# Gelu of the expert layer written to 32-bit buffers in SBUF in place of PSUM, and four buffers for its high and low halves

## The chip, the cores and the metric

The kernel runs on one core of one Trainium2 chip. The metric is the device time of one execution in microseconds. The profile's engines are TensorE (PE, with its weight loads shown apart as PEld), VectorE (DVE), ScalarE (ACT), GpSimd (POOL) and SyncE (SP, which here only issues DMAs).

## What is computed

The reference is a small hybrid of convolution and attention over an input of 4 batches, 128 channels and 32 x 32 positions, so 4 x 1024 tokens of 128 values. Cut to what matters:

```python
x = conv_attention(x, theta_w, phi_w, proj_w)          # softmax(theta x . phi x) applied to x, projected, added
t = tokens(x)                                          # 4 x 1024 tokens of 128
t = t + attention(layernorm(t), Wk, bk, Wq, bq, Wv, bv)
xf = layernorm(t)                                      # the expert layer
top_w, top_i = top_k(xf @ Wg + bg, 2)                  # two of eight experts for each token
for e in range(8):
    h = gelu(xf @ W1[e] + b1[e])                       # 128 -> 512
    out += w_dense[:, e] * (h @ W2[e] + b2[e])         # 512 -> 128
t = t + out
```

The change lies in the expert layer alone.

## The kernel before

Products are made with 16-bit operands: a 32-bit value is held as a high half (its 16-bit rounding) and a low half (what the rounding left), and the products of the halves are summed.

**Attention stage.** The first two thirds of the program run eight attention units, pipelined over steps. There DVE makes the low halves of the exponentials at line 1784 and line 1791 (`EL <- E, EH`: a 32-bit buffer in SBUF less a 16-bit buffer in SBUF), and at line 1860 low halves of weights from SBUF buffers. Towards its end POOL sends the normalised tokens to a buffer in memory (`zbuf`), sorted by expert: function `scatter`, line 605, one indirect DMA for each of 64 groups of 128 rows, whose row numbers (`posi`) lie in SBUF.

**Expert stage.** The tokens sorted by expert are worked through in 36 tiles, `j` from 0 to 35: the first 28 tiles (`WHOLE`) have 256 rows of one expert, the last 8 are pairs of half tiles of 128 rows, each with an expert of its own. For each tile

- SP loads the rows into one of eight buffers (`load_tile`, line 486);
- PE turns them (`rows_T`, line 1092), and ACT copies them to SBUF (`rows_T`, line 1241);
- PE makes the hidden layer (`hidden`, line 1116) in one of two PSUM buffers, `WIDE[0]` (named SC in the trace) and `WIDE[1]` (named PV);
- ACT applies Gelu in place in PSUM (line 1483) and then copies the result to the high half `hh` (line 1489; the trace shows it as line 1213, `EH <- SC` or `EH <- PV`);
- DVE makes the low half `hl` (`low_halves`, line 2038): the Gelu in PSUM less the high half in SBUF. I call this instruction the low of tile j;
- PE makes the output product (`output`, line 1135) in PSUM (MX), two tiles behind the hidden layer;
- DVE sums the parts of the product (`output`, line 2040; the reduction is line 2052) into one of 24 buffers, and makes the row numbers (`yid`, line 2048);
- POOL sends each half of 128 rows to its rows in memory (`ybuf`; function `put`, line 727, indirect DMA of line 731). I call one such DMA a put: two for each tile, 71 in all, as the last tile has one half.

**What sets the order.** Every engine runs a list that is written out by hand, and semaphores tie them. PE's list is `hidden(j)`, `output(j - 2)`, `rows_T(j + 2)`. ACT's is Gelu of j, high half of j, `rows_T(j + 2)`. DVE's is low of j, output of j - 2, and for j up to 12 some small instructions that make the tables of the next tiles (lines 1649 to 1720). POOL's is first the scatters of the last two batches, then the puts in the order of the tiles.

**Waits around the change.** `hidden(j)` writes over the PSUM buffer that low of j - 2 reads, so it waits for that low (`hl_ready`, line 1123). High and low halves have two buffers, so the high half of j and low of j wait for the output product of j - 2 (`y_full`, lines 1488 and 2034). `output(j)` on PE waits for low of j, and for the reduction of j - 2 (`y_ready`).

**The end.** SP loads the results back by parts (`load_outputs`, line 504): the first part once tiles 0 to 31 are written, the second with tile 32, and so on to tile 35. DVE and ACT weigh and add them (`mix_half`, line 2059, lines 2055 and 2068; `mix_quarter`), PE turns the sums, ACT copies and SP stores them.

Of the kernel before, what the change touches and what calls it, by code (L numbers as in the profile page):

```python
# [20 lines left out]
F32 = mybir.dt.float32  # L21
F16 = mybir.dt.float16
# [4 lines left out]
ACT = mybir.ActivationFunctionType  # L27
AX = mybir.AxisListType

P = 128  # L30
B = 4
S = 1024
T = S // P
# [6 lines left out]
WS = 64.0  # L40
HALF = 512
VW = P + 1
# [6 lines left out]
HC = HID // P  # L49
TR = 2 * P  # L50
# [9 lines left out]
NT = WHOLE + REST // 2  # L60
# [2 lines left out]
PADS = E + E  # L63
IN_BUFS = 8
Y_BUFS = 24


def build(nc, x, theta_w, phi_w, proj_w, Wk, bk, Wq, bq, Wv, bv, Wg, bg, W1, b1, W2, b2, out):
    ds = bass.ds
    with ExitStack() as ctx:  # L70
        def sb(name, shape, dt):
            return ctx.enter_context(nc.sbuf_tensor(name, shape, dt))
# [4 lines left out]
        def sem(name):  # L77
# [8 lines left out]
        ZN = ZZ[:, :, 2 * P:ROW].bitcast(I32)  # L86
        QK = sb("QK", [P, 3, 4, S], F16)
        QH, QL, KH, KL = (QK[:, :, j, :] for j in range(4))
        VH = sb("VH", [P, 4, T, VW], F16)
        VL = sb("VL", [P, 4, T, P], F16)  # L90
        EH = sb("EH", [P, 2, T, S], F16)
        EL = sb("EL", [P, 2, T, S], F16)
# [59 lines left out]
        EH0, EH1 = (EH[:, j].rearrange("p a b -> p (a b)") for j in range(2))  # L152
# [32 lines left out]
        Xg = Xw.rearrange("p (g d) -> p g d", g=E * HC)  # L185
        tin = EH0[:, 0:IN_BUFS * 2 * ROW].rearrange("p (b q r) -> p b q r", q=2, r=ROW)
        zT = EH0[:, IN_BUFS * 2 * ROW:IN_BUFS * 2 * ROW + 4 * TR].rearrange("p (b h r) -> p b h r", b=2, h=2)
        hh, hl = (EH1[:, at:at + 2 * HC * TR].rearrange("p (b r) -> p b r", b=2)
                  for at in (4 * TR, 4 * TR + 2 * HC * TR))
        y32 = [t.bitcast(F32)[:, TR * b:TR * (b + 1)].rearrange("p (q c) -> p q c", q=2)  # L190
               for t in (EL0, QK0[:, 8 * S:]) for b in range(t.shape[1] // (2 * TR))]
        yid = sb("yid", [P, Y_BUFS, 2], U32)
# [15 lines left out]
        WIDE = [t[:].rearrange("p b n -> p (b n)") for t in (SC, PV)]  # L208
# [75 lines left out]
        h_ready = sem("h_ready")  # L284
        hh_ready = sem("hh_ready")
        hl_ready = sem("hl_ready")
        y_full = sem("y_full")
# [452 lines left out]
        def _(pe):  # L740
            def mm(o, w, r, start, stop):
                return nc.tensor.matmul(o, w, r, start=start, stop=stop)  # L742
# [7 lines left out]
            for s in STEPS:  # L750
                u, a, m, v = roles(s)
# [364 lines left out]
            def hidden(j):  # L1116

                if j > 0 and listed_at(j, 0) % E == 0:
                    load_experts(listed_at(j, 0) // E)
                b = j % 2  # L1120
                pe.wait_ge(zt_ready, j + 1)
                if j >= 2:
                    pe.wait_ge(hl_ready, j - 1)
                for q in (None,) if j < WHOLE else halves(j):
                    e = expert(j, q)
                    r = slice(0, TR) if q is None else slice(q * P, (q + 1) * P)
                    for c in range(HC):
                        o_ = WIDE[b][:, c * TR:(c + 1) * TR][:, r]
                        w = ds(e * HID + c * P, P)
                        mm(o_, W1H[:, w], zT[:, b, 0, r], True, False)  # L1130
                        mm(o_, W1H[:, w], zT[:, b, 1, r], False, False)
                        last = mm(o_, W1L[:, w], zT[:, b, 0, r], False, True)
                last.then_inc(h_full, 1)

            def output(j):

                b = j % 2
                pe.wait_ge(hl_ready, j + 1)
                if j >= 2:
                    pe.wait_ge(y_ready, j - 1)  # L1140
                for q in halves(j):
                    if q == 0 or j >= WHOLE:
                        e = expert(j, q)
                        both = [W2HL[:, ds(e * HC + c, 1), :, :] for c in range(HC)]
                        mine = pick[:, ds(e, 1), :]
                    o_ = MX[:, b * HALF + q * TR:b * HALF + (q + 1) * TR]
                    for c in range(HC):
                        k = slice(c * TR + q * P, c * TR + (q + 1) * P)
                        if c < HC - 1:
                            mm(o_, hh[:, b, k], both[c], c == 0, False)  # L1150
                            mm(o_[:, 0:P], hl[:, b, k], both[c][:, :, 0, :], False, False)
                        else:
                            mm(o_[:, 0:P], hl[:, b, k], both[c][:, :, 0, :], False, False)
                            mm(o_[:, 0:P], mine, B2[:], False, False)
                            last = mm(o_, hh[:, b, k], both[c], False, True)
                last.then_inc(y_full, 1)

            pe.wait_ge(table_ready, 2)
# [16 lines left out]
            for j in range(2, NT):  # L1175
                if j == FIRST:
                    pe.wait_ge(table_ready, 4)
                if j == FIRST + SECOND:
                    pe.wait_ge(table_ready, 6)
                if listed_at(j, 0) // E == WHOLE // E:  # L1180
                    pe.wait_ge(table_ready, 8)
                hidden(j)
                if j == 2:
                    pe.wait_ge(last_logits_read, 1)
                    pe.wait_ge(wexp_lo, 2 * PAIRS)
                    pe.wait_ge(b2_ready, 1)
                    pe.wait_ge(picks_made, 2)
                if j == 3:
                    pe.wait_ge(rank_read, B)
                output(j - 2)  # L1190
                if j + 2 < NT:
                    rows_T(j + 2)
            for j in (NT - 2, NT - 1):
                output(j)


# [14 lines left out]
        def _(act):  # L1211
# [34 lines left out]
            for s in STEPS:  # L1246
                u, a, m, v = roles(s)
# [230 lines left out]
            def gelu(j):  # L1478
                b = j % 2
                act.wait_ge(h_full, j + 1)  # L1480
                r = slice(0, len(halves(j)) * P)
                h_, high = (o.rearrange("p (c r) -> p c r", c=HC)[:, :, r] for o in (WIDE[b], hh[:, b, :]))
                nc.scalar.activation(h_, h_, ACT.Gelu, scale=1 / WS).then_inc(h_ready, 1)

                act.wait_ge(h_ready, j + 1)
                if j >= 2:

                    act.wait_ge(y_full, j - 1)
                cp(high, h_).then_inc(hh_ready, 1)

            for j in range(NT):
# [30 lines left out]
        def _(dve):  # L1522
# [506 lines left out]
            def low_halves(j):  # L2029
                b = j % 2  # L2030
                dve.wait_ge(hh_ready, j + 1)
                if j >= 2:

                    dve.wait_ge(y_full, j - 1)
                r = slice(0, len(halves(j)) * P)
                h_, high, low_ = (o.rearrange("p (c r) -> p c r", c=HC)[:, :, r]
                                  for o in (WIDE[b], hh[:, b, :], hl[:, b, :]))
                nc.vector.tensor_tensor(low_, h_, high, ALU.subtract).then_inc(hl_ready, 1)  # L2038

            def output(j):  # L2040
# [49 lines left out]
            picks(B - 1)  # L2090
            for j in range(NT):
                low_halves(j)
                if j >= 2:
                    output(j - 2)
                if j == 0:
                    place(B - 1)
                    nc.vector.tensor_copy(padrow[:], start[:]).then_inc(pad_ready, 1)
                if j == 1:
                    not_done()
                    segment_ends(E)  # L2100
                    segments_past(SECOND, E)
                    segment_jumps(SECOND, E)
                if j == 2:
                    summed_past(FIRST, SECOND, E)
                    summed_jumps(FIRST, SECOND, E)
                    listed(FIRST, SECOND, E)
                if j == 3:
                    taken(SECOND)
                if j == 4:
                    counted_tiles(whole_tiles[:], ALU.is_gt, P, TR)  # L2110
                    counted_tiles(total[:], ALU.is_gt, 0, P)
                if j == 5:
                    third_tiles()
                    segment_ends(2 * E)
                if j == 6:
                    segments_past(THIRD, 2 * E)
                    segment_jumps(THIRD, 2 * E)
                if j == 7:
                    summed_past(FIRST + SECOND, THIRD, 2 * E)
                    summed_jumps(FIRST + SECOND, THIRD, 2 * E)  # L2120
                    listed(FIRST + SECOND, THIRD, 2 * E)
                if j == 9:
                    taken(THIRD, 2 * E)
                if j == 10:
                    last_halves()
                    segment_ends(2 * E)
                if j == 11:
                    segments_past(REST, 2 * E)
                    segment_jumps(REST, 2 * E)
                if j == 12:  # L2130
                    summed_past(WHOLE, REST, 2 * E)
                    summed_jumps(WHOLE, REST, 2 * E)
                    listed(WHOLE, REST, 2 * E)
                if j == 15:
                    weigh(1, slice(0, (B - 1) * T))
                    nc.vector.memset(spare[:], 0.0).then_inc(weighed, 1)
            for j in (NT - 2, NT - 1):
                output(j)
            for k in range(2 * (B - 1)):
                mix_half(k)  # L2140
# [28 lines left out]
```

## Time and profile before

| | us |
|---|---|
| median of three runs | 466.13 (466.06 to 467.18) |
| the profiled execution | 465.63 |
| its span, first to last instruction | 463.9 |

| engine | busy us | share of the span |
|---|---|---|
| PE (matmul) | 382.6 | 82% |
| DVE | 360.7 | 78% |
| ACT | 331.2 | 71% |
| POOL | 301.3 | 65% |

The shares are averages over the attention stage, the expert stage (first Gelu at 319.46 us of the span, last put issued at 442.24 us) and the end. The granted TensorE clock is 1.00 of full speed from 330 us to 438 us and 0.50 from 322 us to 326 us; these are its levels of 2.4 and 1.2 GHz. A line of the timeline gives the start, the duration, the engine, the line of the kernel, the operation, output and inputs by name, the shape, and in brackets how long the engine had been idle before it and what released it.

### The profile page before, as it was taken

Reading aid. Unit: us, or ns where it says so; the run is one execution under the profiler, and the core shown is the slowest. Engines: PE = TensorE matmul, PEld = TensorE weight load, DVE = VectorE, ACT = ScalarE, POOL = GpSimd, SP = SyncE. Lnnn points to the kernel's source line nnn. Section 1 sums busy time; section 2 is a strip of 40 time slices with the busy share of each in tenths; the row PEclk is TensorE's granted clock in tenths of the full one; section 3 lists DMA queues with packets and bytes.
Section 4 is the critical chain, followed back from the end, with each engine's and each line's share of the span. In section 5 each row is a group of like instructions: output and inputs, shape, how many; then the busy total and the mean of one; then the engine's idle time right before and its main releaser. Section 6 shows DMA issues by size and latency. Waiting matters only on the chain. (4 is left out here: it accounts for less than half of the span.)

```text
span 463.9 us, 12169 instructions
## 1 busy us (share of the span) xinstructions
PE 382.6 (82%) x3919; PEld 287.0 (62%) x3919; DVE 360.7 (78%) x1024; ACT 331.2 (71%) x650; POOL 301.3 (65%) x304
## 2 busy tenths in 40 slices
PE   4777679997999989999959677466999999999534
PEld 3443356675666756767737455464889899987422
DVE  3795789998889898989797289687898876655656
ACT  4687958785896867877748487459678888866553
POOL 9423834776877776575658857767777777775510
PEclk9997999998999999999999799888999999999955
DMA  6006022200000000002300010133244333331386
GB/s 217 10 12 172 2 46 91 95 3 2 0 2 1 2 1 2 1 2 78 105 7 27 29 36 30 48 88 99 71 116 112 107 92 103 100 94 46 81 273 244
DMA packets 31775, 30.67 MB, mean 66 GB/s; under 512 B 8678, under 2 KB 24953, under 8 KB 31721
## 3 DMA queue, kind: packets, MB, share of 16 engines
q1 hardware_dynamic: 27402, 21.05, 16.4%
q0 software_dynamic: 4320, 8.92, 5.8%
q8 instruction: 32, 0.52, 0.5%
q14 instruction: 21, 0.17, 0.1%
HBM read 17.87 MB, written 12.08 MB: 65 GB/s over the span
## 5 line engine op out<-in xcount | busy, mean ns | idle before, releaser
L1302 ACT ACTIVATE E<-SC 128x512 f32<-128x512 f32 x128 | 77.3, 604 | 44.1 <-PE SC L742 41.4
L742 PE MATMUL PV<-VH,EH 128*128 128x129 f16 x512 | 97.4, 229 | 5.9 <-DVE TOK L1803 5.9
L742 PE MATMUL SC<-QK 128*128 128x512 f16 x326 | 92.1, 389 | 9.3 <-ACT EH L1303 3.2
L742 PE MATMUL PV<-VH,EL 128*128 128x129 f16 x512 | 97.1, 226 | 0.0
L742 PE MATMUL PV<-VL,EH 128*128 128x128 f16 x512 | 97.0, 225 | 0.0
L605 POOL DMA_INDIRECT zbuf<-ZZ,posi x64 | 68.3, 1068 | 25.0 <-issue 17.9
L1761 DVE TENSOR_REDUCE mx<-MX 128x1 f32<-128x1024 f32 x56 | 68.1, 1217 | 19.1 <-PE MX L742 19.0
L1303 ACT ACTIVATE EH<-SC 128x512 f16<-128x512 f32 (+1 forms) x128 | 77.6, 606 | 0.0
L657 POOL TENSOR_TENSOR EL<-E,EH 128x1024 f16<-128x1024 f32 (+1 forms) x28 | 59.6, 2128 | 12.9 <-ACT EH L1303 12.7
L731 POOL DMA_INDIRECT ybuf<-EL,yid x55 | 53.3, 969 | 21.9 <-issue 14.0
L742 PEld LDWEIGHTS PV<-VH,EH 128*128 128x128 f16 (+1 forms) x512 | 51.8, 101 | 12.1 <-issue 6.1
L742 PE MATMUL MX<-QK,EH 128*128 x568 | 56.7, 246 | 1.4 <-DVE EL L2052 1.1
L742 PEld LDWEIGHTS PV<-VL,EH 128*128 128x128 f16 (+1 forms) x512 | 52.6, 103 | 5.1 <-issue 0.8
L742 PEld LDWEIGHTS PV<-VH,EL 128*128 128x128 f16 (+1 forms) x512 | 51.3, 100 | 0.4
L742 PEld LDWEIGHTS MX<-QK,EH 128*128 128x128 f16 x568 | 47.1, 98 | 6.7 <-issue 2.7
L742 PEld LDWEIGHTS SC<-QK 128*128 128x128 f16 (+1 forms) x326 | 28.4, 100 | 33.7 <-issue 7.7
L636 POOL TENSOR_TENSOR ZZ<-ZC,rstd 128x254 f16<-128x254 f32 (+1 forms) x24 | 14.6, 609 | 49.1 <-DVE rstd L1825 48.9
L1784 DVE TENSOR_TENSOR EL<-E,EH 128x1024 f16<-128x1024 f32 x28 | 38.3, 1367 | 10.3 <-ACT EH L1303 10.1
L742 PE MATMUL MX<-QK 128*128 128x512 f16 x122 | 38.0, 394 | 9.1 <-DVE mx L1761 6.5
L2038 DVE TENSOR_TENSOR EH<-SC,EH 128x1024 f16<-128x1024 f32 x18 | 22.0, 1224 | 15.9 <-ACT EH L1213 15.9
L1213 ACT ACTIVATE QK<-PR 128x256 f16<-128x256 f32 (+5 forms) x56 | 25.5, 456 | 10.4 <-PE PR L742 10.3
L2038 DVE TENSOR_TENSOR EH<-PV,EH 128x1024 f16<-128x1024 f32 (+1 forms) x18 | 21.5, 1192 | 12.7 <-ACT EH L1213 12.6
(254 smaller groups left out, 891.6 us busy)
## 6 DMA issues: line engine op xcount, KB each, us to landing
EH<-zbuf SPq DMA_DIRECT2D x28, 130.0 KB
X<-in_x_dram SPq DMA_DIRECT2D x4, 512.0 KB, 5.1
X<-in_L_ffn_W_dram SPq DMA_DIRECT2D x1, 2048.0 KB
EL<-ybuf SPq DMA_DIRECT2D x4, 512.0 KB, 4.2
out_dram<-X SPq DMA_DIRECT2D x8, 256.0 KB, 3.5
W1H<-in_L_ffn_W_dram SPq DMA_DIRECT2D x4, 256.0 KB, 4.6
W1L<-in_L_ffn_W_dram SPq DMA_DIRECT2D x4, 256.0 KB, 6.2
zbuf<-zer SPq DMA_DIRECT2D x16, 64.0 KB, 1.8
```

The lines of the kernel that those rows point to most:

```text
L605: nc.gpsimd.indirect_dma_start(out=zbuf, out_offset=bass.IndirectOffsetOnAxis(ap=posi[:, q, t:t + 1], axis=0), in_=ZZ[:, t, :], in_offset= ...
L636: nc.gpsimd.tensor_tensor(ZZ[:, t, 1:P], ZC[:, :, 1:P], wide(rstd[:, a_ % 2, k], 1), ALU.mult)
L657: nc.gpsimd.tensor_tensor(EL[:, w % 2, ds(i * 2, 2), c], E32h[1], EH[:, w % 2, ds(i * 2, 2), c], ALU.subtract).then_inc(e32_free[1], 1)
L731: nc.gpsimd.indirect_dma_start(out=ybuf, out_offset=bass.IndirectOffsetOnAxis(ap=yid[:, b, q:q + 1], axis=0), in_=y32[b][:, q, :], in_offs ...
L742: return nc.tensor.matmul(o, w, r, start=start, stop=stop)
L1213: return nc.scalar.activation(o, i_, ACT.Copy, scale=scale)
L1302: nc.scalar.activation(E32h[h][:, p, :], SC[:, p, :], ACT.Exp, scale=sc)
L1303: nc.scalar.activation(EH[:, x % 2, ds(i * 2 + p, 1), c], SC[:, p, :], ACT.Exp, scale=sc) \
L1761: nc.vector.reduce_max(mx[:, t:t + 1], MX[:], AX.X).then_inc(mx_free, 1)
L1784: nc.vector.tensor_tensor(EL[:, u % 2, ds(i * 2, 2), c], E32h[0], EH[:, u % 2, ds(i * 2, 2), c], ALU.subtract).then_inc(e32_free[0], 1)
L2038: nc.vector.tensor_tensor(low_, h_, high, ALU.subtract).then_inc(hl_ready, 1)
```

## The change

Gelu's output goes from PSUM to SBUF: two 32-bit buffers `H32`, laid over the values of attention (`VH`), which nobody reads any more by then. High and low halves get four buffers in place of two (`H_BUFS`). So `hidden(j)` waits only for Gelu of j - 2 (`h_ready`), Gelu of j waits for low of j - 2 (`hl_ready`, the last reader of its buffer), and the high half and low of j wait for the output product of j - 4. The low now reads two SBUF buffers. `LAG` is 2, as the distance of the output products was before.

No instruction is moved on any engine: the lists of PE, ACT, DVE, POOL and SP have the same rows in the same order, and only operands and waits differ. The diff, cut to its core:

```diff
+H_BUFS = 4
+LAG = 2
-        VH = sb("VH", [P, 4, T, VW], F16)
+        VHF = sb("VHF", [P, 4 * T * VW], F16)
+        VH = VHF[:].rearrange("p (a t c) -> p a t c", a=4, t=T)
-        hh, hl = (EH1[:, at:at + 2 * HC * TR].rearrange("p (b r) -> p b r", b=2)
-                  for at in (4 * TR, 4 * TR + 2 * HC * TR))
+        hh, hl = (EH1[:, at:at + H_BUFS * HC * TR].rearrange("p (b r) -> p b r", b=H_BUFS)
+                  for at in (0, H_BUFS * HC * TR))
+        VH0 = VHF[:].bitcast(F32)
+        H32 = [VH0[:, b * HC * TR:(b + 1) * HC * TR] for b in range(2)]
@@ hidden(j) on PE
-                    pe.wait_ge(hl_ready, j - 1)
+                    pe.wait_ge(h_ready, j - 1)
@@ output(j) on PE
-                b = j % 2
+                b, d = j % 2, j % H_BUFS
-                            mm(o_, hh[:, b, k], both[c], c == 0, False)
+                            mm(o_, hh[:, d, k], both[c], c == 0, False)
...
@@ gelu(j) on ACT
-                h_, high = (o.rearrange("p (c r) -> p c r", c=HC)[:, :, r] for o in (WIDE[b], hh[:, b, :]))
-                nc.scalar.activation(h_, h_, ACT.Gelu, scale=1 / WS).then_inc(h_ready, 1)
+                sums, h_, high = (o.rearrange("p (c r) -> p c r", c=HC)[:, :, r]
+                                  for o in (WIDE[b], H32[b], hh[:, j % H_BUFS, :]))
+                if j >= 2:
+                    act.wait_ge(hl_ready, j - 1)
+                nc.scalar.activation(h_, sums, ACT.Gelu, scale=1 / WS).then_inc(h_ready, 1)
                 act.wait_ge(h_ready, j + 1)
-                if j >= 2:
-                    act.wait_ge(y_full, j - 1)
+                if j >= H_BUFS:
+                    act.wait_ge(y_full, j - H_BUFS + 1)
                 cp(high, h_).then_inc(hh_ready, 1)
@@ low_halves(j) on DVE
-                if j >= 2:
-                    dve.wait_ge(y_full, j - 1)
+                if j >= H_BUFS:
+                    dve.wait_ge(y_full, j - H_BUFS + 1)
                 h_, high, low_ = (o.rearrange("p (c r) -> p c r", c=HC)[:, :, r]
-                                  for o in (WIDE[b], hh[:, b, :], hl[:, b, :]))
+                                  for o in (H32[b], hh[:, j % H_BUFS, :], hl[:, j % H_BUFS, :]))
                 nc.vector.tensor_tensor(low_, h_, high, ALU.subtract).then_inc(hl_ready, 1)
```

## Rows read from the trace of the kernel before

**Rows 1.** Busy time by window: us, PE, PEld, DVE, ACT, POOL, clock, DMA share, GB/s

```profile
366.00:370.00 4.00, 4.00 (x45) 3.67 (x44) 2.35 (x5) 3.50 (x5) 3.09 (x4) 1.00 0.35 101
```

**Rows 2.** Waits, 319 to 438 us: who for whom, total us, times, longest

```profile
POOL ybuf L731 <- DVE EL L2052: 7.6, 8, 2.3
...
PE MX L742 <- DVE EL L2052: 1.1, 1, 1.1
PE SC L742 <- DVE EH L2038: 1.0, 2, 0.6
...
PE PV L742 <- DVE EH L2038: 0.7, 2, 0.4
```

**Rows 3.** Timeline: high half of tile 34 on ACT, reduction of tile 32 on DVE

```profile
431.15 1.02 ACT L1213 ACTIVATE EH<-SC 128x1024 f16<-128x1024 f32 x1 [1.03 <-PE MX L742]
...
433.61 0.68 DVE L2052 TENSOR_REDUCE EL<-MX 128x256 f32<-128x512 f32 x1
```

**Rows 4.** Timeline of POOL: puts 1, 58, 65 and 70 of 71

```profile
347.92 0.97 POOL L731 DMA_INDIRECT ybuf<-EL,yid  x1 [0.30 <-DVE EL L2052]
...
420.50 0.97 POOL L731 DMA_INDIRECT ybuf<-EL,yid  x1 [0.30 <-issue]
...
434.56 0.97 POOL L731 DMA_INDIRECT ybuf<-EL,yid  x1 [2.34 <-DVE EL L2052]
...
440.96 0.97 POOL L731 DMA_INDIRECT ybuf<-EL,yid  x1 [0.31 <-issue]
```

**Rows 5.** Timeline of the end: DVE on the fourth part, ACT's last copy

```profile
449.35 1.14 DVE L2055 SCALAR_TENSOR_TENSOR TOK<-EL,WT,TOK 128x128 f32<-128x128 f32 x4 [0.47 <-DMA EL<-ybuf]
...
460.83 0.60 ACT L1213 ACTIVATE X<-PV 128x512 f32<-128x512 f32 x1 [1.50 <-PE PV L1205]
```

**Rows 6.** Timeline: POOL's scatters beside DVE instructions with two SBUF inputs

```profile
244.57 1.21 DVE L1784 TENSOR_TENSOR EL<-E,EH 128x1024 f16<-128x1024 f32 x1
245.34 1.28 POOL L605 DMA_INDIRECT zbuf<-ZZ,posi  x1 [0.30 <-issue]
...
281.07 1.19 DVE L1860 SCALAR_TENSOR_TENSOR QK<-X,QK 128x1024 f16<-128x1024 f32 x1
281.30 1.80 POOL L605 DMA_INDIRECT zbuf<-ZZ,posi  x1 [0.30 <-issue]
282.18 1.22 DVE L1784 TENSOR_TENSOR EL<-E,EH 128x1024 f16<-128x1024 f32 x1
...
338.71 0.42 DVE L1651 TENSOR_TENSOR W0b<-cnt,half_ends 128x256 f32<-128x256 f32 x1
...
338.90 1.08 POOL L605 DMA_INDIRECT zbuf<-ZZ,posi  x1 [0.30 <-issue]
```

**Rows 7.** Timeline: lows of tiles 19 and 20, and a put during the first

```profile
381.77 1.22 DVE L2038 TENSOR_TENSOR EH<-PV,EH 128x1024 f16<-128x1024 f32 x1 [1.01 <-ACT EH L1213]
382.30 0.97 POOL L731 DMA_INDIRECT ybuf<-EL,yid  x1 [0.30 <-issue]
384.74 1.22 DVE L2038 TENSOR_TENSOR EH<-SC,EH 128x1024 f16<-128x1024 f32 x1 [1.01 <-ACT EH L1213]
```

**Rows 8.** Timeline of DVE: lows of tiles 32 and 33, half tiles

```profile
423.83 1.23 DVE L2038 TENSOR_TENSOR EH<-SC,EH 128x1024 f16<-128x1024 f32 x1 [1.81 <-ACT EH L1213]
...
427.63 1.22 DVE L2038 TENSOR_TENSOR EH<-PV,EH 128x1024 f16<-128x1024 f32 x1 [1.72 <-ACT EH L1213]
```

**Rows 9.** Timeline: a put that begins 0.04 us after a two-input DVE instruction

```profile
439.65 0.76 DVE L2068 TENSOR_TENSOR TOK<-TOK,EL 128x512 f32<-128x512 f32 x1 [0.33 <-ACT EL L1213]
439.69 0.97 POOL L731 DMA_INDIRECT ybuf<-EL,yid  x1 [0.30 <-issue]
```

**Rows 10.** Groups of instructions: count, busy us and mean ns, idle before them

```profile
L1213 ACT ACTIVATE EH<-SC 128x1024 f16<-128x1024 f32 x18 | 18.4, 1023 | 9.7 <-PE MX L742 9.7
L1483 ACT ACTIVATE SC<-SC 128x1024 f32<-128x1024 f32 x18 | 18.2, 1009 | 5.7 <-PE SC L742 5.7
...
L1213 ACT ACTIVATE X<-X 128x1024 f16<-128x1024 f32 x4 | 4.2, 1058 | 1.0 <-DMA X<-in_x_dram 0.9
```

More of the change, by code:

```diff
@@ L1149, in output @@
                         if c < HC - 1:
-                            mm(o_, hh[:, b, k], both[c], c == 0, False)
-                            mm(o_[:, 0:P], hl[:, b, k], both[c][:, :, 0, :], False, False)
+                            mm(o_, hh[:, d, k], both[c], c == 0, False)
+                            mm(o_[:, 0:P], hl[:, d, k], both[c][:, :, 0, :], False, False)
                         else:
-                            mm(o_[:, 0:P], hl[:, b, k], both[c][:, :, 0, :], False, False)
+                            mm(o_[:, 0:P], hl[:, d, k], both[c][:, :, 0, :], False, False)
                             mm(o_[:, 0:P], mine, B2[:], False, False)
-                            last = mm(o_, hh[:, b, k], both[c], False, True)
+                            last = mm(o_, hh[:, d, k], both[c], False, True)
                 last.then_inc(y_full, 1)
@@ L1182, in _ @@
                 hidden(j)
-                if j == 2:
+                if j == LAG:
                     pe.wait_ge(last_logits_read, 1)
@@ L1187, in _ @@
                     pe.wait_ge(picks_made, 2)
-                if j == 3:
+                if j == LAG + 1:
                     pe.wait_ge(rank_read, B)
-                output(j - 2)
+                if j >= LAG:
+                    output(j - LAG)
                 if j + 2 < NT:
                     rows_T(j + 2)
-            for j in (NT - 2, NT - 1):
+            for j in range(NT - LAG, NT):
                 output(j)
@@ L2092, in _ @@
                 low_halves(j)
-                if j >= 2:
-                    output(j - 2)
+                if j >= LAG:
+                    output(j - LAG)
                 if j == 0:
@@ L2136, in _ @@
                     nc.vector.memset(spare[:], 0.0).then_inc(weighed, 1)
-            for j in (NT - 2, NT - 1):
+            for j in range(NT - LAG, NT):
                 output(j)
```

## The prediction

> **What bounds the kernel now.** I read the busy time by windows first. In the middle of the expert stage PE is busy all of the time at the full granted clock [rows 1], so a tile costs what its matmuls cost, 2.97 us (the lows of tiles 19 and 20 start at 381.77 and 384.74 [rows 7]). Then the waits of that stage: PE loses little to the lows, 1.0 + 0.7 = 1.7 us in four waits, and 1.1 us in one wait at the end for a reduction [rows 2]. These are what the change can give PE.
>
> Then the end, followed back. The last copy ends at 461.4. DVE starts on the fourth part at 449.35, released by a DMA [rows 5], and that part is loaded once tile 34 is written, that is behind put 70, which ends at 441.93 [rows 4]: 7.4 us from put to DVE, and 12.1 us more to the end. So the stream of puts on POOL sets the end, not PE. The reader is to see three stretches of that stream [rows 4]. From put 1 at 347.92 (late, since the scatters come first) to put 58 at 420.50 POOL never catches up: 57 cycles in 72.58 us, 1.273 us each, of which 0.97 is the DMA instruction and 0.30 the step to the next. Then it has caught up and waits for reductions: 8 waits, 7.6 us [rows 2], less the usual 0.30 of each, is 5.2 us of spare time. From 434.56 the last seven puts run in a row. So 5.2 us is all the cover that POOL has: what slows the puts by more than that moves the end.
>
> **The change part by part.** *Waits on PE.* `hidden(j)` now waits for a Gelu that is long done, not for a low, and the 1.7 us go. `output(j)` still needs the low, but 12 matmuls later. *Waits on ACT and DVE.* The high half of tile 34 no longer waits 1.03 us for the output product [rows 3]; its low follows, and behind that on DVE the reduction of tile 32 at 433.61, for which put 65 and PE both wait [rows 2, 4]. It comes 1.0 us earlier. Together reductions at the end come 1.7 + 1.0 = 2.7 us earlier. That is worth 2.7 us if the puts follow.
>
> *The added wait.* Gelu of j waits for low of j - 2. Queued behind it on ACT are the high half of j and the copy of the turned rows, for which `hidden(j + 2)` waits. But low of 19 ends at 382.99, and Gelu of 21 comes on ACT behind the high half of 20, which releases the low at 384.74 [rows 7]: the low is done 1.8 us before it is asked for. Nothing.
>
> *ACT's operands.* A copy of 128x1024 from SBUF takes 1058 ns, from PSUM 1023 [rows 10]: 36 x 0.035 = 1.3 us more on ACT at the most. Gelu into SBUF I bound by the row for PSUM to PSUM, 1009 ns, and the one for PSUM to SBUF, 1023 ns: 0 to 0.5 us. ACT has some 0.5 us of waiting in each tile (9.7 us before 18 high halves, for the output product, a wait that goes [rows 10]), so I cost both at nothing; without that cover 1.8 us.
>
> *The low's operands, the term that decides.* The low had one input in PSUM and one in SBUF; now both lie in SBUF. Its own time stays: the same shapes from SBUF take 1.22 us at 282.18 [rows 6], as now [rows 7]. But look at POOL beside such instructions [rows 6]. A scatter, the same instruction form as a put, takes 0.97 us alone. The one at 245.34 takes 1.28, the one at 281.30 takes 1.80, the one at 338.90 takes 1.08. Each began while a DVE instruction with two SBUF inputs ran, and each ends 0.84 us after that instruction does: 245.78 + 0.84, 282.26 + 0.84, 339.13 + 0.85. There are twelve such scatters, all with 0.83 to 0.86. So in its first 0.97 - 0.84 = 0.13 us a scatter needs something that such an instruction holds, presumably for its list of row numbers in SBUF; later it needs it no more (the instruction that began at 282.18, in the middle of the scatter, delayed nothing). With PSUM as one input there is none of this: the put at 382.30 starts in the middle of a low and takes 0.97 [rows 7].
>
> So from the first low on, every put or scatter that starts in the first 1.22 - 0.13 = 1.09 us of a low runs as if begun at 1.09. Follow one tile: starts at 1.09, 2.36 and 3.64 us after the low's start. The next low starts at 2.97, so the third start is 0.67 into it and is held for 0.42 us, back to 1.09. The pattern repeats: two puts for each tile of 2.97 us in place of two in 2.55. POOL is locked to the lows and cannot catch up. For the 28 whole tiles this is 28 x 0.42 = 11.8 us. (Scatters are held in tiles 0 to 8 and pass the delay on to the puts. The lows up to tile 12 are spaced unevenly, by the small instructions for the tables; I take the same 0.42.)
>
> For half tiles the lows are 3.80 us apart [rows 8]. Three cycles are 3.82, so after 1.09, 2.36 and 3.64 the fourth start is 4.91, which is 1.11 after the next low's start and just free. Depending on jitter none or all of the 7 half-tile lows cost up to 0.42: 0 to 2.9 us. I take 1.2, since the spacings of the first ones differ from 3.80 by more than the 0.02 to spare. Against this stands the spare time of 5.2 us, which is used up first. Sum: 11.8 + 1.2 - 5.2 = 7.8 us later for put 70, and the 7.4 and 12.1 us behind it stay. 465.63 of the profiled execution + 7.8 = 473.4 us. The median of the runs is 0.5 above that execution; I leave this to the range. PE's 2.7 us are lost, since POOL is by then some 8 us behind the reductions.
>
> The Trainium skill, SBUF — State Buffer, Who interferes with whom, says that a VectorE instruction with two SBUF inputs contends with a GpSimd instruction that reads SBUF, and not with one that only writes it. The scatters' delays agree with the first half. The same section says that in a probe tensor_tensor did not stall DMAs issued from GpSimd, as making their descriptors needs the write side only; by that the puts would keep their 0.97 us, and the time would be that of the first rival. The trace speaks against it for an indirect DMA.
>
> **The rivals.** *Puts are not held.* All evidence is from scatters; of puts the trace has one near case, which began 0.04 us after a two-input instruction and took 0.97 [rows 9]. It was first, or 0.04 us is too short. If puts are not held, the end follows the reductions: 465.63 - 2.7 = 462.9, faster. The price that decides: at a hold of x us per tile put 70 moves by 28x - 5.2 us, but not earlier than the reductions allow (-2.7). So from x = 0.19 on the kernel is slower than before. Against this rival stand the same instruction form and the twelve cases. Chance 0.08.
>
> *Held, but not in step.* If the starts fall at random, one in three (0.99 of 2.97 us) meets a low and is held for 0.5 us on average: 0.33 per tile, 28 x 0.33 = 9.3, and nothing in half tiles: + 4.1, 469.7. Against it: a held put starts the next pattern at a fixed place. Chance 0.12.
>
> *Held more.* All 35 lows cost 0.42, 14.7 - 5.2 = + 9.5, 475.1; and the uneven lows up to tile 12, where two holds of up to 0.99 can follow each other, add perhaps 2: 477. Chance 0.12.
>
> *The change doesn't do what it says.* The lows stay late for PE, because Gelu waits for them in place of `hidden`. Then PE keeps its 1.7 us of waits, which costs nothing as POOL ends later anyway: the forecast's time. It is no case of its own.
>
> *It comes out even.* Holds near 0.19 per tile. No row makes that price. Chance 0.03.
>
> **How the numbers follow.** The forecast has 0.65, with 471.5 to 475.5 as its own range (1.2 us for half tiles between 0 and 2.9). Held at random ends at 469.7 and held more at 477, so 468.0 to 477.5 takes both in and leaves out the puts that are not held and the even case, 0.11, and some of the tails. A difference of 0.3% (1.4 us) is about what a measurement of this kernel can tell. Faster by more: 0.08. Within: 0.03. Slower by more: 0.65 + 0.12 + 0.12 = 0.89.
>
> **What would show it.** After the change the lows read `VH` or `VHF` and the high halves, both in SBUF. Right: of each three put starts about one is at 1.1 to 1.8 us with an end 0.84 us after a low's end; the last scatter ends near 351.5 in place of 347.6; put 70 ends near 449.7 and follows put 69 without a wait; PE's last output product ends 2 us earlier than now, and no wait of PE for a low remains. Wrong: all puts at 0.97 us while lows run, and POOL waiting for reductions near the end as it does now; or a second wait behind put 70 that takes the delay up, so that less of it reaches the end.

## The result and the profile after

The median rose from 466.10 to 476.42 us, a ratio of 1.0207 with a 95% interval of 1.0170 to 1.0244. The forecast was 473.4 in a range of 468.0 to 477.5: the sign came as forecast, and the time is 3 us above the forecast, inside its range. One of the six executions of the changed kernel took 628.95 us at a granted clock of 0.56 and is left out of the ratio. The profiled execution took 476.17 us, 10.54 more than that of the kernel before.

The page of the changed kernel, busy time by engine (us and share of the span) and three groups of instructions (count, busy us, mean ns, idle time before them):

```profile
PE 381.7 (80%) x3919; PEld 287.3 (61%) x3919; DVE 361.1 (76%) x1024; ACT 334.0 (70%) x650; POOL 314.8 (66%) x304
...
L610 POOL DMA_INDIRECT zbuf<-ZZ,posi x64 | 72.7, 1136 | 25.0 <-issue 17.9
...
L736 POOL DMA_INDIRECT ybuf<-EL,yid x55 | 60.6, 1102 | 16.8 <-issue 16.5
...
L2048 DVE TENSOR_TENSOR EH<-VHF,EH 128x1024 f16<-128x1024 f32 (+1 forms) x36 | 43.6, 1211 | 24.8 <-ACT EH L1219 24.5
```

Only POOL's busy time grew by much, from 301.3 to 314.8 us. DVE's is the same, and the low takes 1.21 us on average: the instruction that changed its operands pays nothing itself. A put of the group shown takes 1102 ns on average in place of 0.97 us, and what precedes the puts is now the 0.30 us step ("issue"); POOL no longer stands still for a reduction.

The same kernel's timeline of POOL (start, duration) around the lows of tiles 18 and 19, to be held against [rows 7]:

```profile
376.85 0.97 POOL L736 DMA_INDIRECT ybuf<-EL,yid  x1 [0.30 <-issue]
378.12 1.38 POOL L736 DMA_INDIRECT ybuf<-EL,yid  x1 [0.30 <-issue]
379.81 0.97 POOL L736 DMA_INDIRECT ybuf<-EL,yid  x1 [0.30 <-issue]
381.09 1.39 POOL L736 DMA_INDIRECT ybuf<-EL,yid  x1 [0.30 <-issue]
382.78 0.97 POOL L736 DMA_INDIRECT ybuf<-EL,yid  x1 [0.30 <-issue]
```

and of DVE:

```profile
377.44 1.23 DVE L2048 TENSOR_TENSOR EH<-VHF,EH 128x1024 f16<-128x1024 f32 x1 [1.01 <-ACT EH L1219]
...
380.41 1.22 DVE L2048 TENSOR_TENSOR EH<-VHF,EH 128x1024 f16<-128x1024 f32 x1 [1.01 <-ACT EH L1219]
```

This is the locked pattern. The put of 378.12 begins 0.68 us into the low and ends at 379.50, which is 0.83 after the low's end at 378.67. Two cycles later the next one begins at 381.09, 0.68 into the next low. Each tile brings two puts and loses 0.41 to 0.42 us. It holds without a gap from 369 to 412 us.

The ends: the last two scatters, put 70 and the last put on POOL,

```profile
349.52 1.47 POOL L610 DMA_INDIRECT zbuf<-ZZ,posi  x1 [0.30 <-issue]
351.29 1.56 POOL L610 DMA_INDIRECT zbuf<-ZZ,posi  x1 [0.30 <-issue]
...
449.96 1.08 POOL L736 DMA_INDIRECT ybuf<-EL,yid  x1 [0.30 <-issue]
451.35 0.98 POOL L736 DMA_INDIRECT ybuf<-EL,yid  x1 [0.30 <-issue]
```

the fourth part on DVE, and ACT's last copy, which answer to [rows 4, 5]:

```profile
459.26 1.14 DVE L2065 SCALAR_TENSOR_TENSOR TOK<-EL,WT,TOK 128x128 f32<-128x128 f32 x4 [1.61 <-DMA EL<-ybuf]
...
471.29 0.60 ACT L1219 ACTIVATE X<-PV 128x512 f32<-128x512 f32 x1 [1.50 <-PE PV L1211]
```

Put 70 ends at 451.04 (before 441.93), the last copy at 471.89 (before 461.43). And all waits of PE from 319 to 450 us (who for whom, total us, times, longest):

```profile
PE PV L747 <- ACT EH L1219: 1.2, 1, 1.2
PE MX L747 <- DVE picked L1623: 0.9, 1, 0.9
PE SC L747 <- issue: 0.3, 1, 0.3
PE MX L747 <- DVE EL L2062: 0.2, 1, 0.2
```

No wait for a low is left, and of the 1.1 us for a reduction at the end 0.2 remain [rows 2]. PE got what the change was to give it: its last product of the expert stage ends at 434.27 us of the span, before at 436.92.

**Where the 10.54 us went**, in the profiled executions. I count from the start of the first of the last 32 scatters, for which POOL waits in either kernel; from there it pauses no more in the changed kernel, and in the kernel before only ahead of the last puts (5.2 us in all, up to put 65). I call the stretch from there to put 70 the stream. It starts 0.93 us later (307.10, before 306.17). From there to the end of put 70 it takes 143.94 us in place of 135.76, which is 8.2 more. From there to ACT's last copy, which I call the tail, it takes 20.85 in place of 19.50, 1.35 more; the rest, 0.1, is behind that.

### The profile page after: what moved, and what is told of

It is laid out like the page before. It is cut to its first block, busy times and chain, and to the rows that moved or that the text cites. A ratio compares the mean times of both kernels' runs of the same rounds, so it can differ in the third digit from the quotient of the medians.

```text
span 474.3 us, 12200 instructions
## 1 busy us (share of the span) xinstructions
PE 381.7 (80%) x3919; PEld 287.3 (61%) x3919; DVE 361.1 (76%) x1024; ACT 334.0 (70%) x650; POOL 314.8 (66%) x304
## 4 chain that ended last, share of the span: by engine, by line
PE 50%; DVE 20%; POOL 9%; issue 9%; ACT 8%; DMA 3%; SPq 0%; POOLq 0%; ACTq 0%; DVEq 0%
PE PV L747 15%; PE MX L747 14%; PE SC L747 14%; PE PR L747 5%; POOL zbuf L610 4%; DVE mx L1771 3%; DVE EL L1794 3%; POOL ybuf L736 3%; PE PR L1105 2%; ACT EH L1309 1%; ACT E L1308 1%; DMA ybuf<-EL,yid 1%; ACT QK L1219 1%; DMA VL<-ybuf 1%; ACT X L1219 1%
## 5 line engine op out<-in xcount | busy, mean ns | idle before, releaser
L747 PE MATMUL PV<-VHF,EH 128*128 128x129 f16 x512 | 97.5, 229 | 5.9 <-DVE TOK L1813 5.9
L747 PE MATMUL PV<-VHF,EL 128*128 128x129 f16 x512 | 97.3, 226 | 0.0
L610 POOL DMA_INDIRECT zbuf<-ZZ,posi x64 | 72.7, 1136 | 25.0 <-issue 17.9
L736 POOL DMA_INDIRECT ybuf<-EL,yid x55 | 60.6, 1102 | 16.8 <-issue 16.5
L2048 DVE TENSOR_TENSOR EH<-VHF,EH 128x1024 f16<-128x1024 f32 (+1 forms) x36 | 43.6, 1211 | 24.8 <-ACT EH L1219 24.5
L747 PEld LDWEIGHTS PV<-VHF,EH 128*128 128x128 f16 (+1 forms) x512 | 51.8, 101 | 12.6 <-issue 6.3
L747 PEld LDWEIGHTS PV<-VHF,EL 128*128 128x128 f16 (+1 forms) x512 | 51.3, 100 | 0.1
L1219 ACT ACTIVATE EH<-VHF 128x1024 f16<-128x1024 f32 (+1 forms) x36 | 37.6, 1045 | 1.1
L1219 ACT ACTIVATE QK<-PR 128x256 f16<-128x256 f32 (+5 forms) x56 | 25.5, 455 | 10.5 <-PE PR L747 10.4
```

The costliest lines, as they stand in the source:

```text
L610: nc.gpsimd.indirect_dma_start(out=zbuf, out_offset=bass.IndirectOffsetOnAxis(ap=posi[:, q, t:t + 1], axis=0), in_=ZZ[:, t, :], in_offset= ...
L736: nc.gpsimd.indirect_dma_start(out=ybuf, out_offset=bass.IndirectOffsetOnAxis(ap=yid[:, b, q:q + 1], axis=0), in_=y32[b][:, q, :], in_offs ...
L1219: return nc.scalar.activation(o, i_, ACT.Copy, scale=scale)
```

## The experiments

The theory (A, the forecast's): the low with two SBUF inputs holds the put or scatter that starts in its first 1.09 us, POOL falls into step with the lows, and the stream of puts is late. Rivals: the new place of the buffers and the waits and copies that go with it cost the time; the puts are held, but at random and not in step; or the number of buffers is at fault.

**Four buffers alone, Gelu left in PSUM.** Against the changed kernel, cut to its core:

```diff
-                    pe.wait_ge(h_ready, j - 1)
+                    pe.wait_ge(hl_ready, j - 1)
@@ gelu(j): output; low_halves(j): input
-                H32[b]
+                WIDE[b]
-                if j >= 2:
-                    act.wait_ge(hl_ready, j - 1)
```

> One part of the change alone: high and low halves have four buffers, but Gelu stays in place in PSUM and hidden(j) waits for the low of j - 2 as before. Theory A (the puts on POOL are held by lows with two SBUF inputs): no put is held, all take 0.97 us, and the high half of tile 34 no longer waits 1.0 us for an output product, so reductions at the end come about 1.2 us earlier: 465 us, 0.2 to 0.5% faster than the kernel before. Rival B (the four buffers and their waits make the tiles slower): 470 us or more, at least 0.8% slower than before, with new waits on PE, ACT or DVE.

Measured: 463.51 us, ratio 0.9946 (0.9922 to 0.9971). This is faster than both kernels, by somewhat more than expected. From its groups, and its timeline of POOL at put 65:

```profile
L736 POOL DMA_INDIRECT ybuf<-EL,yid x55 | 53.3, 969 | 19.7 <-issue 14.0 <-DVE EL L2059 5.7
```

```profile
432.71 0.97 POOL L736 DMA_INDIRECT ybuf<-EL,yid  x1 [2.06 <-DVE EL L2059]
```

All puts take 0.97 us, and POOL waits for reductions near the end, as before [rows 4]. Of all puts and scatters, 26 start between 0.10 us after the start of a low and 0.13 us before its end; all take 0.97 us. In the changed kernel there are 28 such starts, and every one is held (1.09 to 1.94 us). The operation and the number of inputs are the same; here one input lies in PSUM. Four buffers let the high half of tile 34 and the lows come without the output product, so that put 65 comes 1.85 us earlier. The four buffers and their waits are thus worth 2.6 us. In the profiles the place of Gelu's output, with the waits that go with it, costs 10.5 us in the stream of scatters and puts (143.94 us in the changed kernel, 133.46 here) and 1.3 behind put 70 (20.85, here 19.55), 11.8 in all; the medians differ by 12.9, or by 9.8 with the second measurement of the changed kernel (below).

**Gelu in SBUF, but a low with one input.** The kernel leaves out the subtraction of the high half. Against the changed kernel, cut to its core:

```diff
-                nc.vector.tensor_tensor(low_, h_, high, ALU.subtract)
+                nc.vector.reduce_sum(low_, h_.unsqueeze(3), AX.X)
```

> The kernel after with the low made by a reduction over an axis of length one, so that it reads one SBUF buffer and not two; it leaves out the subtraction of the high half, so its low half is the Gelu rounded to 16 bits. Buffers, waits and the place of Gelu are those of the kernel after. Theory A (held by two SBUF inputs): puts are back at 0.97 us while lows run, and the time is what the waits alone give, 463 to 465 us, some 12 us below the kernel after. Rival B (Gelu to SBUF, ACT's copy from SBUF or the new wait of Gelu is what costs): the time stays at 474 to 477 us. Rival C (POOL is slowed by any DVE instruction that reads SBUF): puts stay at 1.4 us every second time, 474 to 477 us.

Measured: 463.29 us, ratio 0.9935 (0.9909 to 0.9960). From its groups:

```profile
L2049 DVE TENSOR_REDUCE EH<-VHF 128x1024 f16<-128x1024 f32 (+1 forms) x36 | 43.3, 1203 | 24.4 <-ACT EH L1219 24.0
```

```profile
L736 POOL DMA_INDIRECT ybuf<-EL,yid x55 | 53.3, 969 | 17.5 <-issue 15.2 <-DVE EL L2063 2.3
```

The buffers, ACT's copies from SBUF, the added wait and even the low's duration (1203 ns on average) stand as in the changed kernel; the second input is gone, and with it every hold during a low. The operation is another too (a reduction), but the subtraction in the version with Gelu in PSUM, which has one SBUF input, held nothing either. The stream to put 70 takes 131.23 us, 12.7 less than in the changed kernel. So it is not the place of the buffers, and not DVE's time, but the second SBUF input.

**The low in four and in two pieces.** Against the changed kernel, cut to its core, with n = 4 and n = 2:

```diff
+for k in range(n):
+    c = slice(k * HC // n, (k + 1) * HC // n)
+    nc.vector.tensor_tensor(low_[:, c], h_[:, c], high[:, c], ALU.subtract)
```

> The kernel after with each low in four instructions of 128x256, one for each chunk of 256 columns. A start can then be held only until the end of a piece, at most some 0.3 us, which is less than the 0.42 us by which a tile (2.97) is longer than two put cycles (2.55). Theory A, in step: a held start lands ahead of the next low one tile later, POOL is not locked to the tiles and runs nearly free: last scatter near 348.5, put 70 within 1 us of the kernel before, 466 to 468 us. Rival A2 (the whole low blocks POOL whatever its pieces): as the kernel after or, as the low is 0.3 us longer, more, 476 to 478 us.

> The kernel after with each low in two instructions of 128x512. A start is held until the end of a piece, at most some 0.56 us, more than the 0.42 us to spare. Theory A, in step: two puts per tile wherever the pattern locks, in some tiles or all; put 70 some 4 to 8 us later than before, 470 to 474 us. Theory A, starts at random: two pieces of 0.56 us hold 0.21 us per tile on average, 28 x 0.21 = 5.9 against 5.2 us of spare time: 466 to 468 us. Rival A2 (the whole low blocks whatever its pieces): 476 us.

Measured: 465.19 us with four pieces, ratio 0.9978 (0.9947 to 1.0009); 470.18 us with two, ratio 1.0131 (1.0074 to 1.0188). Four pieces, from the groups:

```profile
L2050 DVE TENSOR_TENSOR EH<-VHF,EH 128x256 f16<-128x256 f32 (+1 forms) x144 | 51.1, 417 | 19.8 <-ACT EH L1219 19.2 <-DVE done L1715 0.3
```

```profile
L736 POOL DMA_INDIRECT ybuf<-EL,yid x55 | 55.1, 1003 | 16.8 <-issue 16.5 <-DVE QK L2065 0.3
```

Two inputs as in the changed kernel, and 7.5 us more work on DVE (51.1 against 43.6), and yet 11.2 us faster (8.1 against the second measurement of the changed kernel), 9.2 of them in the stream to put 70: with one exception a put or scatter is held only until the end of the piece that it meets. 33 puts and scatters are held here too, but by 5.03 us in all in place of 14.24. Two pieces, timeline of POOL and of DVE (x2 are the two pieces, the first 0.69 us):

```profile
374.93 1.38 POOL L736 DMA_INDIRECT ybuf<-EL,yid  x1 [0.30 <-issue]
376.62 0.97 POOL L736 DMA_INDIRECT ybuf<-EL,yid  x1 [0.30 <-issue]
377.89 1.39 POOL L736 DMA_INDIRECT ybuf<-EL,yid  x1 [0.31 <-issue]
```

```profile
374.79 1.29 DVE L2050 TENSOR_TENSOR EH<-VHF,EH 128x512 f16<-128x512 f32 x2 [0.94 <-ACT EH L1219]
...
377.75 1.29 DVE L2050 TENSOR_TENSOR EH<-VHF,EH 128x512 f16<-128x512 f32 x2 [0.94 <-ACT EH L1219]
```

This run decides between in step and at random. The put of every tile from 369 to 401 us starts 0.14 us into the low and is held for the same 0.41 us as with whole lows, although the instruction that holds it is little more than half as long. Random starts would have been held less often and shorter, for the 466 to 468 us of that expectation. In step, the loss per tile is set by the tile's period, 2.97 less two cycles of 1.273 us, and not by the length of the instruction, as long as the stretch in which it holds is longer than these 0.42 us. With pieces of 0.42 us it is not (0.42 less 0.13 is 0.29), and the lock is gone. The two pieces still gain 3.4 us over one in the stream (140.52 us), mainly in the first 13 tiles, where the lows are spaced unevenly and no lock stands: the holds there sum to 2.2 us in place of 5.0.

**Gelu in SBUF with two buffers for the halves.** Against the changed kernel:

```diff
-H_BUFS = 4
+H_BUFS = 2
```

> The other part of the change alone: Gelu goes to the 32-bit buffers in SBUF, hidden(j) waits for Gelu, and high and low halves keep two buffers. Theory A (lows with two SBUF inputs hold the puts): every second put takes some 1.4 us in the whole tiles, last scatter and put 70 as late as in the kernel after or up to 1 us later; 475 to 478 us. Rival B (the cost lies in the four buffers or their waits, or only in both parts together): about the time of the kernel before, 463 to 468 us.

Measured: 477.43 us, ratio 1.025 (1.020 to 1.030). From its page:

```profile
L736 POOL DMA_INDIRECT ybuf<-EL,yid x55 | 61.2, 1113 | 16.8 <-issue 16.2
```

34 puts and scatters are held, by 15.86 us in all. ACT waits for output products again, but POOL has no pause in which that would show: four buffers or two, the time follows the holds.

**The cost by itself: an instruction with two SBUF inputs added to the fast version.** Behind the lows of tiles 13 to 27 of the version with Gelu in PSUM, cut to its core, with n = 640 and n = 256:

```diff
+                if 13 <= j < WHOLE:
+                    nc.vector.tensor_tensor(beside[:], VHF[:, 0:2 * n].bitcast(F32),
+                                            VHF[:, 2048:2048 + n], ALU.subtract).then_inc(beside_done, 1)
```

> The kernel of the first run (Gelu in PSUM, four buffers for the halves; 463.5 us) with one added DVE instruction in tiles 13 to 27, behind the low: 128x640, both inputs in SBUF, its result unused. DVE waits 1.0 us in each of these tiles, so DVE has the room. It can hold a start for up to some 0.7 us, more than the 0.42 us to spare. Theory A, in step: POOL is locked to these 15 tiles, 15 x 0.42 = 6.3 us less the 3.0 us that POOL waited for reductions in that run: + 3 us, 466 to 467.5 us. Rival (what costs lies in Gelu's place, ACT's copies or the waits, of which nothing changes here): 463 to 464 us.

> As the run with the added instruction of 128x640, but 128x256: it can hold a start for up to some 0.3 us, less than the 0.42 us to spare. Theory A, in step: POOL is not locked, about one tile in three loses up to 0.3 us, some 1 us in all, which the 3.0 us of POOL's waits cover: 463 to 464 us. Starts at random would give nearly the same here; a hold for any two-input instruction whatever its length would give the 466 to 467.5 us of the longer one.

Measured: 465.61 us with 640 columns, ratio 1.0010 (0.9978 to 1.0042); 464.16 us with 256, ratio 0.9957 (0.9914 to 0.9999). The version without it had 0.9946. The larger one, timeline of POOL:

```profile
378.73 0.97 POOL L738 DMA_INDIRECT ybuf<-EL,yid  x1 [0.30 <-issue]
380.00 1.27 POOL L738 DMA_INDIRECT ybuf<-EL,yid  x1 [0.30 <-issue]
381.58 0.97 POOL L738 DMA_INDIRECT ybuf<-EL,yid  x1 [0.30 <-issue]
382.85 1.38 POOL L738 DMA_INDIRECT ybuf<-EL,yid  x1 [0.30 <-issue]
```

and of DVE:

```profile
379.61 0.81 DVE L2051 TENSOR_TENSOR beside<-VHF 128x640 f16<-128x640 f32 x1
...
382.58 0.81 DVE L2051 TENSOR_TENSOR beside<-VHF 128x640 f16<-128x640 f32 x1
```

An instruction of 0.81 us that nobody waits for locks POOL just as the low does, at 0.27 us from its start, with the same 0.41 us per tile. The end came less late than expected (2.1 us by the medians, 3 expected), since the lock stands for 9 tiles in place of 15: the starts of the puts move by 0.42 us from tile to tile, and only at 380 us do they reach the added instruction. The rows reckon it up: 9 holds by it are 3.6 us, and put 70 is held for 0.16 us by a DVE instruction of the end; of this 2.96 us go into the spare time that POOL had without it, and 0.9 us reach the end of put 70; the tail behind it is 1.1 us longer, as in all the runs without a pause (below). The small one, 0.41 us long, delays no put by more than 0.03 us: only one start fell into its first 0.28 us, and the others, which move by 0.42 us from tile to tile, stepped over that stretch. The stream takes 134.17 us with it, 133.46 without; POOL's pauses for reductions are longer by as much (3.61 us, without it 2.95), so that the 0.7 us are not holds. So a two-input instruction that returns in every tile costs much only where it is long enough for the lock.

**The changed kernel once more.** No edit.

> The kernel after, once more, for its size: 7.8 us were forecast and 10.3 measured. In its first profile the input arrived 0.9 us later than in the profile of before, the puts lost 8.2 us and the loads behind the last puts 1.4 us. If the late input was chance, the expert stage starts at another time here and the median ratio falls to 1.017 to 1.020; if the loads' 1.4 us belong to the change, the time from the end of put 70 to DVE's fourth part is again near 8.2 us, and not 7.4.

Measured: 473.27 us, ratio 1.0171 (1.0110 to 1.0233). The stream to put 70 takes 143.86 us, as in the first profile (143.94), with 32 holds of 14.29 us; from put 70 to the last copy it takes 20.73 (20.85), and to DVE's fourth part 7.97, nearer to the 8.2 of the first profile than to the 7.4 of the kernel before. What differs is where the stream starts: 303.96 us in place of 307.10. That lies ahead of the expert stage, and with it ahead of everything that the change touches; over all the profiled kernels here this start lies between 303.95 and 308.02. Stream and tail together cost 9.5 us in the first profile and 9.3 in the second, against the profile of the kernel before. By the profiles the two measurements, 10.32 and 7.55 us, differ by that start: 0.93 us later than in the kernel before in the first profile, 2.21 earlier in the second. What makes it move is left open.

## Why the prediction was right, and where its sizes were off

**PE's waits go, and the gain is lost.** Right. The four waits for the low are gone, PE's last product ends 2.65 us earlier (forecast 2), or 3.6 counted from the first Gelu, which came 0.94 later, and nothing comes of it, because POOL pauses for no reduction any more. So this term was real and covered only by the late puts, but the 2.7 us by which reductions were to come earlier were too small. The run with one input has the whole term without a hold by a low: there put 65 starts 123.90 us behind the start of the stream, before 128.39, and the stream is 4.5 us shorter. The version with Gelu in PSUM, in which PE still waits 1.0 us for lows, has 2.3 us of this, on ACT and DVE; that its median is 2.6 us lower, near the 2.7, is chance.

**The added wait and ACT's operands at nothing.** Right: the run with one input has both, and is the fastest measured with the version in PSUM (463.29 and 463.51).

**The low keeps its time, and POOL pays.** Right, and the term by size:

| us | forecast | changed kernel |
|---|---|---|
| held in the first 13 whole tiles | 5.5 | 5.0 (11 holds, 2 of them by instructions for the tables) |
| held in the other 15 whole tiles | 6.3 | 6.8 (15 holds) |
| held in half tiles | 1.2 (0 to 2.9) | 1.4 (4 holds) |
| POOL's spare time | -5.2 | -5.2 |
| put 70 later than its stream's start | 7.8 | 8.2 |

The rows above the last sum to 8.0 us; the other 0.2 stand in no row here. The two rows of whole tiles split the forecast's 11.8 us as 13 and 15 times 0.42. That their sum came out at 11.8 is partly luck: the uneven lows of the first 13 tiles were held 0.5 us less than I took, and two starts ahead of the lock 0.64 and 0.78 us. In the half tiles the reason was another than I gave: not jitter of the fourth start, but the first two lows, which still come 3.0 us after one another as in whole tiles (0.45 us each), and the last two; in between the starts fall from 0.06 us ahead of a low's start to 0.01 us behind it, and none is held. The last scatter ended at 352.85 us, forecast 351.5, and put 70 at 451.04, forecast 449.7; 0.93 of each difference is the later start of the stream. One sign I had put down wrongly: "about one of three" put starts late. The forecast's own pattern, two puts per tile of which the second meets the next low, makes it one of two, and in the locked stretch it is one of two; over all 71 puts it is 22, as few are held behind that stretch.

The section "Who interferes with whom" of the Trainium skill, SBUF — State Buffer, says that DVE instructions with two SBUF inputs contend with GpSimd's reads of SBUF, and that trn2's tensor_reduce never does. The runs agree: 28 of the 33 holds are by lows with the subtraction; with the reduction of the same duration there are two holds, both outside the lows. Where it says that in a probe tensor_tensor did not stall DMAs issued from GpSimd, these indirect DMAs differ, and the measurement decides.

**The step that was mis-sized: "the 7.4 and 12.1 us behind it stay".** They do not: from put 70 to the fourth part it takes 8.22 us and from there 12.63, together 1.35 more (1.2 in the second profile). Timeline of the kernel before, put 66 on POOL and the second part on DVE, which is loaded behind put 66:

```profile
435.84 0.97 POOL L731 DMA_INDIRECT ybuf<-EL,yid  x1 [0.30 <-issue]
```

```profile
442.71 1.14 DVE L2055 SCALAR_TENSOR_TENSOR TOK<-EL,WT,TOK 128x128 f32<-128x128 f32 x4 [2.31 <-DMA EL<-ybuf]
```

and the same two in the changed kernel:

```profile
444.85 0.97 POOL L736 DMA_INDIRECT ybuf<-EL,yid  x1 [0.30 <-issue]
```

```profile
453.65 1.14 DVE L2065 SCALAR_TENSOR_TENSOR TOK<-EL,WT,TOK 128x128 f32<-128x128 f32 x4 [2.17 <-DMA EL<-ybuf]
```

From put 66's end to the part it is 5.90 us before and 7.83 after. Before, POOL paused 2.34 us ahead of put 65 [rows 4], so that the load of the first part (512 KB), which waits for put 64, had 4.59 us from the end of that put to the end of put 66; without the pause it has 2.54. The trace has the landings: the first part lands at 438.16 before and at 449.30 after, put 66 right behind it at 438.52 and 449.51 (2.7 and 4.7 us after its start), and SP issues the second load only then. Put 70 in the same way takes 3.9 us to land before and 5.2 after. Nine of the ten profiles fit it: the three whose POOL pauses 2.05 to 2.34 us ahead of put 65 take 19.5 to 19.75 us from put 70 to the last copy, the six without a pause 20.6 to 20.95. The run with one input does not: it pauses there for 1.05 us and takes longest, 21.33, since its put 70 needs 6.2 us to land; why is open. That it is the loads is read from rows; no run took that cause away by itself. The forecast should have seen it: it let the pauses go from the stream, and left what they spaced out as it was.

**The rest of the difference.** 0.93 us of the first profile is the later start of the stream, which was 2.2 us earlier in the second. The sum, 465.63 + 0.93 + 8.2 + 1.35 + 0.1 = 476.2, is the profiled execution.

**The rivals.** *Puts are not held* (462.9) is out by the 22 held puts, beside 11 held scatters. Its number is close to what the versions without holds by lows do take, 463.3 and 463.5, in part by luck: with one input the stream is 4.5 us shorter than before and the tail 1.8 us longer, neither of which it had. *At random* is out by the fixed 0.68 us from low to put in the changed kernel and by the run with two pieces. Its price was too low: it took 0.99 us of each low where the working of the forecast has 1.09, with which two starts per tile lose 0.40 us on average and the time is 471.6 us, inside the forecast's own range. The time alone could not have told the two apart. *Held more*: its time (475.1 to 477) covers what was measured, but not its reason, since the lows of the first 13 tiles were held less than I took, and not more. The near case of [rows 9], 0.04 us after a two-input instruction, is of a kind with the starts that are not held in the last section.

## What to carry to other kernels

Before an operand is moved from PSUM to SBUF, count the SBUF inputs of each DVE instruction that reads it: its own time may stay the same to 0.01 us, while indirect DMAs on POOL beside it are held. Here this cost 10 to 13 us: 473.3 and 476.4 us with the holds, 463.3 and 463.5 without, where the kernel before took 466. A holder that returns with a fixed period can lock a stream that is only a little faster than that period to it; then the loss per period is the stream's whole lead, and making the holder shorter is worth little until it is shorter than that lead. Look at the engine with a stream of fixed work and little spare time, not only at the one whose waits the change removes; and where a pause goes out of a stream, ask what it had spaced out further on.

## What the runs showed that was not expected

A hold depends on the start by hundredths of a microsecond. In the changed kernel, timeline of DVE and of POOL, a low and a scatter 0.13 us behind it:

```profile
343.21 1.23 DVE L2048 TENSOR_TENSOR EH<-VHF,EH 128x1024 f16<-128x1024 f32 x1
```

```profile
343.34 1.94 POOL L610 DMA_INDIRECT zbuf<-ZZ,posi  x1 [0.30 <-issue]
```

and a low and a put 0.01 us behind it:

```profile
417.57 1.27 DVE L2048 TENSOR_TENSOR EH<-VHF,EH 128x1024 f16<-128x1024 f32 x1 [1.69 <-ACT EH L1219]
```

```profile
417.58 0.97 POOL L736 DMA_INDIRECT ybuf<-QK,yid  x1 [0.30 <-issue]
```

The first is held for the whole low and takes 1.94 us, twice its time. The second takes its 0.97, and it is the low that takes 1.27 in place of 1.23. In the runs with Gelu in SBUF, starts 0.10 us into a whole low or later were held, except in its last 0.13 us, and those up to 0.01 us were not; between the two there was none. The scatters of the attention stage narrow it: the one at 253.69 in the changed kernel starts 0.09 us into an instruction with two SBUF inputs and takes 1.97 us, the one at 253.13 in the version with Gelu in PSUM 0.06 us into its own and takes 2.00. Starts at 0.03 to 0.07 us are found held and not held, so no sharp limit can be given. It looks as if whoever reads first goes first, and as if the indirect DMA is then done with its reading early in its 0.97 us: the put delays the low by 0.04 us, and a low delays a put or scatter by up to 1.00 (1.97 us at 350.75 in the run with two buffers).

That an instruction cut in pieces lets POOL in between them was not certain either: with four pieces back to back on DVE all holds by lows but one were under 0.3 us. The one, 0.58 us, began during the third piece and lasted to the end of the fourth, so the change from one piece to the next doesn't always let POOL through. Why is open.
